# Layer norm, transposes and gate of the last four chunks five passes ahead; the top-k search spread over passes 11 to 15

## The reference

```python
xn = layernorm(x)                                    # eps 1e-5, no scale
# attention: windows of 64 rows, 16 heads of 32
qkv = xw @ qkv_w + qkv_b
attn = softmax(q @ k.T * 32**-0.5 + rel_pos_bias)    # 64 x 64 for each window and head
attention = (attn @ v) @ proj_w + proj_b
# experts: each of the 8 experts picks its own 1024 rows
scores = (xn @ Wg.T).T                               # 8 x 8192
top_vals, token_idx = top_k(scores, 1024)
token_w = softmax(top_vals)
h = silu(xg @ W1.T) * (xg @ W3.T)                    # 1024 x 1024 for each expert
y = (h @ W2.T) * token_w
out = x + attention + scatter_add(y)
```

## Time and profile before

| | us |
|---|---|
| median of 3 runs | 2164.89 (2163.88 to 2164.94) |
| profiled execution | 2163.89 |
| its span | 2162.1 |
| TensorE busy | 2082.4 (96%) |
| VectorE busy | 1101.4 (51%) |
| ScalarE busy | 666.6 (31%) |
| GpSimd busy | 517.9 (24%) |

### The profile page before, as it was taken

How to read it: one execution, slowest core, us unless ns; L and a number is a source line. 1 busy time by engine, 2 the same in 40 slices (tenths; PEclk the granted TensorE clock), 3 DMA queues, 4 the chain that set the end, 5 groups by cost and what they waited for, 6 DMA issues and landing times.

```text
span 2162.1 us, 38085 instructions
## 1 busy us (share of the span) xinstructions
PE 2082.4 (96%) x15667; PEld 1680.8 (78%) x15667; DVE 1101.4 (51%) x1652; ACT 666.6 (31%) x1027; POOL 517.9 (24%) x308
## 2 busy tenths in 40 slices
PE   7999999999999999975799999999999999999997
PEld 5877777787777777754688888888888888888886
DVE  6666666565666666688744433343334433344211
ACT  3333332323232333334323332232232322324221
POOL 2333323333333333213111112111220211201111
PEclk9999999999999999986899999999999999999999
DMA  6121222222122112201333233142331423313311
GB/s 216 45 74 46 79 79 79 78 79 71 56 71 79 60 59 79 78 21 40 118 88 106 59 78 97 41 114 59 74 92 49 108 67 68 88 58 89 66 20 20
DMA packets 65749, 159.21 MB, mean 74 GB/s; under 512 B 5565, under 2 KB 5949, under 8 KB 65693
## 3 DMA queue, kind: packets, MB, share of 16 engines
q1 hardware_dynamic: 51356, 124.93, 17.0%
q0 software_dynamic: 14336, 33.56, 8.7%
HBM read 107.09 MB, written 51.31 MB: 73 GB/s over the span
## 4 chain that ended last, share of the span: by engine, by line
PE 51%; DVE 0%; POOL 0%; ACT 0%; issue 0%; POOLq 0%
PE ps_e L53 16%; PE ps_e L54 16%; PE ps_e L55 16%; PE ps_e L1324 1%; PE ps_e L135 1%; POOL out_rows L1228 0%; DVE xgt_lo L1394 0%; ACT x_res L1296 0%; DVE w_lo L1389 0%; ACT w_hi L1264 0%; POOLq L1227 0%
## 5 line engine op out<-in xcount | busy, mean ns | idle before, releaser
L53 PE MATMUL ps_e<-xgt_hi,w_hi 128*128 128x512 f32 x1024 | 403.7, 394 | 2.8 <-DVE xgt_lo L1394 2.8
L55 PE MATMUL ps_e<-xgt_hi,w_lo 128*128 128x512 f32 x1024 | 398.6, 389 | 0.0
L54 PE MATMUL ps_e<-xgt_lo,w_hi 128*128 128x512 f32 x1024 | 398.5, 389 | 0.0
L1414 DVE TENSOR_TENSOR hm<-ps_e,silu 128x512 f32<-128x512 f32 x128 | 88.5, 691 | 531.3 <-PE ps_e L55 530.6
L53 PEld LDWEIGHTS ps_e<-xgt_hi,w_hi 128*128 128x128 f32 x1024 | 192.2, 188 | 40.9 <-DVE xgt_lo L1394 3.0
L55 PEld LDWEIGHTS ps_e<-xgt_hi,w_lo 128*128 128x128 f32 x1024 | 192.2, 188 | 40.5
L164 POOL DMA_INDIRECT x_in<-xn_rows,idx x64 | 75.7, 1183 | 615.9 <-issue 230.2
L54 PEld LDWEIGHTS ps_e<-xgt_lo,w_hi 128*128 128x128 f32 x1024 | 192.4, 188 | 37.9
L53 PE MATMUL ps<-xt_hi,wqk_hi 128*128 128x512 f32 x512 | 212.0, 414 | 0.0
L1284 ACT ACTIVATE h_hi<-hm 128x512 fp32r<-128x512 f32 x128 | 80.9, 632 | 391.6 <-DVE hm L1414 388.7
L54 PE MATMUL ps<-xt_lo,wqk_hi 128*128 128x512 f32 x512 | 201.5, 394 | 0.0
(11 more groups left out here) (166 smaller groups left out, 3585.0 us busy)
## 6 DMA issues: line engine op xcount, KB each, us to landing
xn<-in_w SPq DMA_DIRECT2D x48, 512.0 KB, 3.3
raw<-in_w SPq DMA_DIRECT2D x48, 512.0 KB
xn_rows<-xn SPq DMA_DIRECT2D x16, 1024.0 KB, 5.2
x_res<-in_x SPq DMA_DIRECT2D x16, 1024.0 KB, 5.0
out_rows<-x_res SPq DMA_DIRECT2D x16, 1024.0 KB, 4.2
x_in<-in_x SPq DMA_DIRECT2D x15, 1024.0 KB, 7.2
x_res<-in_wqk SPq DMA_DIRECT2D x3, 512.0 KB, 6.8
x_in<-in_x SPq DMA_DIRECT2D x2, 512.0 KB, 4.1
```

The source lines that it names most:

```text
L53: nc.tensor.matmul(out, w_hi, x_hi, start=start, stop=False)
L54: nc.tensor.matmul(out, w_hi, x_lo, start=False, stop=False)
L55: return nc.tensor.matmul(out, w_lo, x_hi, start=False, stop=stop)
L1414: v.tensor_tensor(hm[:, m % 2, :], ps[:, 2 * (m % 2) + 1, :], silu[:, m % 2, :], ALU.mult).then_inc(hm_ready, 1)
```

## The change

FAR = 12, LEAD = 5, HUNT = 11. Passes 1 to 6 stay a loop, 7 to 14 are written out. In passes 7 to 10 the norm of chunk c+5 (chunks 12 to 15) is done beside that of chunk c+1, in tiles of its own (`x_f`, `xt_f`), and its transposes and gate (`xt_ahead` in passes 7 to 10, `gate_ahead` in passes 8 to 11, four fp32 matmuls for the former 16); its normed rows are stored, and read back into `xn` one pass before they are transposed again for the projections. Passes 11 to 14 have no norm of their own and passes 12 to 15 no gate. `gate_s`, `above` and the rest lie in the memory of `x_f` and `xt_f`. The search's rounds stand at slots n = 1 to 6 of passes 11 to 13, at the same places of every engine's queue (`hunt(c, n)`); slot n = 7 takes the bits of round n = 6. The banks of the counts change with the slot (SLOT_BANK), and TensorE waits with `bank_free` until VectorE has read them. The choice stands in slot 6 of pass 13 to slot 2 of pass 14, positions and weights in slots 2 to 7 of pass 14, the first list's matmuls between the projections of the last pass, and the gather between two softmax steps of GpSimd there. The last output projection is in two parts, three quarters of it before the last group's probabilities are there. On ScalarE the copies of the odd head pairs in the last pass go to VectorE. Cut to what the prediction speaks of, indented eight columns less:

```diff
+FAR = 12
+LEAD = 5
+HUNT = FAR - 1
+ROUNDS = 16
...
+FINAL_BANK = (7, QB, KB, 2)
+SLOT_BANK = (None, QB, KB, KB, KB, QB, 2)
+TOTAL, WGT_T, LISTS = QB, QB, 7
+def slot(c, n):
+    return 6 * (c - HUNT) + n - 2
...
# SyncE's queue
+    def load_xn_back(c):
+        sp.wait_ge(xn_stored, 16 * FAR)
+        sp.wait_ge(xnf_stored, 16 * (c - FAR + 1))
+        sp.wait_ge(xt_mm, KC * c)
+        sp.dma_start(xn[:, :, :], d["xn"][c]).then_inc(xn_back, 16)
+    def load_terms():
+        sp.wait_ge(gate_stored, 64 * FAR)
+        sp.wait_ge(gatef_stored, 64 * (NCH - FAR))
+        sp.wait_ge(xnf_stored, 16 * (NCH - FAR))
+        for j, term in enumerate((gate_s, above, ties, upto)):
+            sp.dma_start(term, d["gate"][j, :, :]).then_inc(scores_in, 16)
...
+    for c in range(FAR - LEAD, NCH - 1):
+        if c < FAR:
+            keep_scores(c)
+        if FAR <= c - 1 + LEAD < NCH:
+            keep_scores_ahead(c - 1 + LEAD)
+        if c == HUNT:
+            load_terms()
+        if c + 1 < FAR:
+            keep_xn(c + 1)
+        else:
+            load_xn_back(c + 1)
+        if c + 2 < FAR:
+            load_x(c + 2)
+        store_out(c - 1)
+        load_res(c)
+        if c + LEAD < NCH:
+            keep_xn_ahead(c + LEAD)
+        if c + LEAD + 1 < NCH:
+            sp.wait_ge(xnf_stored, 16 * (c + LEAD - FAR + 1))
+            load_x_ahead(c + LEAD + 1)
     sp.wait_ge(xt_mm, KC * NCH)
     for u in range(2):
         sp.dma_start(lists.raw[u], d["w13"][0, u]).then_inc(lists.w_in[u], 16)
+    store_out(NCH - 2)
...
# GpSimd's queue
+        if isinstance(c, int) and FAR <= c + LEAD < NCH:
+            layernorm_rstd_ahead(c + LEAD)
+        if isinstance(c, int) and c == NCH - 2:
+            for j in range(2):
+                pool.wait_ge(wgt_part_ready, j + 1)
+                nc.gpsimd.tensor_tensor(lists.wgt[:, :, :], lists.wgt[:, :, :], lists.wgt_parts[:, :, :, j],
+                                        ALU.subtract).then_inc(wgt_rest_ready, 1)
+        if isinstance(c, int) and c == NCH - 1:
+            pool.wait_ge(xn_ready, TT * FAR)
+            pool.wait_ge(xn_stored, 16 * FAR)
+            pool.wait_ge(xnf_stored, 16 * (NCH - FAR))
+            pool.wait_ge(lists.idx_ready, 1)
+            gather(nc, pool, lists, d["xn_rows"], 0, 0)
         softmax(G * c + 2)
...
# ScalarE: of the new hunt() and chunk()
+        if n <= 6 and 0 <= slot(c, n) < ROUNDS:
+            count_hits(slot(c, n))
+        if c == NCH - 3 and n == 6:
+            act.wait_ge(top_ready, 1)
+            nc.scalar.activation(exps, gate_s, ACT.Exp, bias=top[:, 0:1]).then_inc(exps_ready, 1)
+        if c == NCH - 2 and n == 3:
+            take_weights()
+        if c == NCH - 2 and n in (4, 6, 7):
+            weight_part((4, 6, 7).index(n))
...
# TensorE
+    def xt_ahead(j, k):
+        if k == 0:
+            pe.wait_ge(xnf_ready, TT * (j - FAR + 1))
+            pe.wait_ge(out_ready, TT * (j - LEAD))
+        elif k == 1:
+            pe.wait_ge(s_ready, G * (j - LEAD) + 3)
+        elif k == 3:
+            pe.wait_ge(xtf_ready, KC * (j - FAR) + 1)
+        for t in range(TT):
+            i = nc.tensor.transpose(ps[:, F_BANK[k], P * t:P * (t + 1)], x_f[:, t, P * k:P * (k + 1)], ident[:, :])
+        i.then_inc(xtf_mm, 1)
+    def gate_ahead(j):
+        pe.wait_ge(xtf_ready, KC * (j - FAR + 1))
+        pe.wait_ge(s_ready, G * (j - LEAD + 1))
+        for k in range(KC):
+            i = nc.tensor.matmul(ps[32 * k:32 * (k + 1), GF_BANK, :], wg[:, k, :], xt_f[:, k, :], start=True, stop=True)
+        i.then_inc(gatef_mm, 1)
...
+    def project_out_most(c, t):
+        for k in range(KC - 1):
+            split3(nc, ps[:, FINAL_BANK[t], :], ot_hi[:, k, P * t:P * (t + 1)], ot_lo[:, k, P * t:P * (t + 1)],
+                   wp_hi[:, k, :], wp_lo[:, k, :], k == 0, False)
+    def project_out_rest(c, t):
+        k = KC - 1
+        split3(nc, ps[:, FINAL_BANK[t], :], ot_hi[:, k, P * t:P * (t + 1)], ot_lo[:, k, P * t:P * (t + 1)],
+               wp_hi[:, k, :], wp_lo[:, k, :], False, True).then_inc(p_mm, 1)
...
# TensorE's hunt(c, n)
+        s, i, bank = G * c, slot(c, n), SLOT_BANK[n]
+        if i < 0 or (c == NCH - 2 and n > 3):
+            return
+        if n == 1:
+            pe.wait_ge(q_ready, s + 2)
+        elif n <= 4:
+            pe.wait_ge(k_ready, s + 2)
+        elif n == 5:
+            pe.wait_ge(q_ready, s + 3)
+        else:
+            pe.wait_ge(s_ready, s + 3)
+        if c == NCH - 4 and n in (3, 4):
+            pe.wait_ge(bank_read, i)
+        if i < ROUNDS:
+            pe.wait_ge(part_counts, i + 1)
+            pe.wait_ge(hits_summed, 2 * (i + 1))
+            row_matmul(ps[:, bank, 0:3], same[:, :], cnt[:, :]).then_inc(count_mm, 1)
...
+    def bank_free(c, n):
+        if isinstance(c, int) and HUNT <= c < NCH - 1 and slot(c, n) >= 0:
+            pe.wait_ge(bank_read, slot(c, n) + 1)
     def chunk(c, first=False):
         s = G * c
+        ahead = isinstance(c, int) and FAR <= c + LEAD < NCH
+        late = isinstance(c, int) and c >= FAR
         project_q(s, 0, c)
+        if isinstance(c, int) and FAR < c + LEAD <= NCH:
+            gate_ahead(c - 1 + LEAD)
         if not first:
             probs_t(s - 2)
         project_k(s, 0)
         if not first:
             pv(s - 2, 2)
-            gate(c)
+            if not late:
+                gate(c)
...
         project_q(s + 1, 1)
         if not first:
             project_v(c, 0)
+            hunt(c, 1)
             probs_t(s - 1)
         project_k(s + 1, 1)
         if not first:
...
+        hunt(c, 2)
         project_v(c, 2)
         project_v(c, 3)
+        hunt(c, 3)
         pe.wait_ge(v_ready, TT * c + 3)
         scores(s + 1)
         if not first:
-            for t in range(TT - 1):
-                project_out(c - 1, t)
+            project_out(c - 1, 0)
+            project_out(c - 1, 1)
+            hunt(c, 4)
+            project_out(c - 1, 2)
+        bank_free(c, 1)
+        if isinstance(c, int) and c == NCH - 2:
+            pe.wait_ge(wgt_copied, 1)
         project_q(s + 2, 2)
         probs_t(s)
         pe.wait_ge(v_ready, TT * (c + 1))
+        bank_free(c, 2 if isinstance(c, int) and c == NCH - 2 else 4)
         project_k(s + 2, 2)
         pv(s, 0)
+        hunt(c, 5)
         if not first:
             project_out(c - 1, TT - 1)
             pe.wait_ge(out_ready, TT * (c - 1) + 3)
+        scores(s + 2)
+        if not isinstance(c, int) or c < NCH - 2:
+            bank_free(c, 5)
+        project_q(s + 3, 3)
+        hunt(c, 6)
+        if ahead:
+            for k in range(KC - 1):
+                xt_ahead(c + LEAD, k)
+        probs_t(s + 1)
+        if ahead:
+            xt_ahead(c + LEAD, KC - 1)
+        project_k(s + 3, 3)
+        if ahead:
+            pe.wait_ge(xtf_ready, KC * (c + LEAD - FAR + 1))
+        xt(c + 1)
+        if not isinstance(c, int) or c < NCH - 2:
+            bank_free(c, 6)
+        scores(s + 3)
+        pe.wait_ge(xt_ready, KC * (c + 1) + 1)
+        pv(s + 1, 1)
...
# TensorE's last pass, as it is after
+        def lists_of(*groups):
+            for g in groups:
+                compact(nc, pe, lists, ps[:, LISTS, :], 0, g)
+        project_q(s, 0, c)
+        probs_t(s - 2)
+        project_k(s, 0)
+        pv(s - 2, 2)
+        scores(s)
+        project_q(s + 1, 1)
+        project_v(c, 0, last=True)
+        probs_t(s - 1)
+        project_k(s + 1, 1)
+        pv(s - 1, 3)
+        project_v(c, 1, last=True)
+        project_v(c, 2, last=True)
+        lists_of(0, 1)
+        project_v(c, 3, last=True)
+        lists_of(2)
+        pe.wait_ge(v_ready, TT * (c + 1))
+        scores(s + 1)
+        for t in range(TT):
+            project_out(c - 1, t, last=True)
+            lists_of(3 + t)
+        project_q(s + 2, 2)
+        lists_of(7)
+        probs_t(s)
+        project_k(s + 2, 2)
+        pv(s, 0)
+        pe.wait_ge(out_ready, TT * c)
         scores(s + 2)
         project_q(s + 3, 3)
         probs_t(s + 1)
         project_k(s + 3, 3)
         scores(s + 3)
         pv(s + 1, 1)
+        pe.wait_ge(lists.got_ready, 1)
+        pe.wait_ge(q_ready, G * NCH)
+        pe.wait_ge(k_ready, G * NCH)
         probs_t(s + 2)
         pv(s + 2, 2)
+        pe.wait_ge(o_ready, G * NCH - 1)
         for t in range(TT):
+            project_out_most(c, t)
         probs_t(s + 3)
+        pv(s + 3, 3)
+        pe.wait_ge(o_ready, G * NCH)
         for t in range(TT):
+            project_out_rest(c, t)
...
# VectorE
+    def take_bits(i, bank, top_too=False):
+        dve.wait_ge(count_mm, i + 1)
+        reached = v.tensor_scalar(reach[:, :], ps[:, bank, 0:3], float(CAP), 0.0, ALU.is_ge, ALU.add, accum_out=kept[:, :])
+        if top_too:
+            then(reached)
+        else:
+            then_read(reached, i)
+        then(v.tensor_copy(kept_i[:, :], kept[:, :]))
...
# VectorE's hunt(c, n)
+        i = slot(c, n)
...
```

(75 more changed lines are left out.)

520 lines of the change are left out of this document (261 added, 259 removed).

## The result

The changed kernel takes 2178.74 us (median of 4 runs, 2177.03 to 2181.07), the kernel before 2164.43 (4 runs, 2163.88 to 2164.94): ratio 1.0067, 95% interval 1.0049 to 1.0084. It is slower. The profiled execution took 2177.03 us, its span 2175.3, against a span of 2162.1 before. The expert stage now starts at 1066.56 us instead of 1053.56: the 13.0 us between the two are nearly the whole difference of the spans, 13.2.

What follows compares the result with a forecast made beforehand. TensorE bounds passes 1 to 14; the chain of search, choice and list bounds the last. 2163.9 - 55 + 12 + 2.4 - 5.5 + 7.1 + 33.2 + 21.2 = 2179 us, slower; range 2146 to 2202.

Steps and rivals of the forecast that it cites:

- The last pass, -55: Search, choice and most list waits leave the last pass: 99 us against 153.8, bounds 90 and 108.
- The gap: Last pass: GpSimd gathers between softmax(61) and softmax(62), so TensorE waits 5 us for the normalised tile.
- Passes 7 to 10, +12: The second norm there: 1.84 us of transposes a pass plus waits of 1.15, together 3.0 a pass.
- three of the four gate_ahead: Early gate matmuls in passes 8 to 11, 0.59 us each pass, +2.4 in all; three fall in passes 8 to 10.
- Passes 11 to 14: +56.6: Search matmuls +7.1, gate gone -5.5, slot 2 with clock +33.2, other slots +21.2, and pass 11's gate_ahead.
- The waits at slot 2: Passes 11 to 14: search blocked behind GpSimd's residual addition, 6.6 us in passes 12 and 13; with clock +33.2 in all.
- The other slots: Passes 11 to 13: waits at slots 3, 4, 6, project_q and the pass end, +21.2 us, bounds 0 and 35.
- The clock was forecast at 6.8: Passes 11 to 14: matmuls behind each slot 2 wait run at half clock, 1.7 us a pass.
- The lock: VectorE and GpSimd share a port pair exclusively for a whole instruction; by it the 33.2 us at slot 2 stand.
- rival 1: Faster: the residual addition does not meet the search at slot 2, the 33.2 us vanish, 2146 us; chance 0.27.
- The break-even: Slot 2, passes 11 to 14: below 4.4 us a pass, clock included, the change wins.
- Rival 2: Waits of 1 to 2 us in passes 11 to 13 cost clock too, 24 us more: 2203 us; chance 0.10.

Runs made afterwards that it cites:

- the nine variants above: Nine follow-up variants of the changed kernel, altering or moving its bias addition, comparisons, slot 4, gather or key; medians from 2155.90 to 2181.92 us.
- Experiments 1 to 4: Changed kernel without bias addition in passes 11 to 14, 2164.68 us; addition moved, 2167.68; comparisons over 64 of 512 columns, 2171.08; kernel before without addition, 2164.09.
- the late gather: First list's gather put behind the softmax of group 63 instead of between those of groups 61 and 62; alone on the changed kernel, 2181.92 us.
- two pairs: Gather late against early: with addition moved, slot 4 before maximum, key behind xt_lo, 2155.90 against 2160.07 us; with last-pass additions moved too, 2156.37 against 2160.36.
- the third: Changed kernel with only the gather moved behind the last softmax, 2181.92 us, against the changed kernel, 2178.74.

## Why the prediction was right

The forecast was 2179, the time 2178.74, and most terms stood. That they agree to 0.3 us is luck: the four executions lie between 2177.03 and 2181.07, and several errors of 1 to 5 us cancelled. Step by step:

**The last pass, -55: measured -59.0.** Idle 17.5, busy 77.3 at clock 0.96. Two points failed. The gap was forecast at 5 us before probs_t(62), with TensorE waiting for the normalised tile; it is 3.96 before scores(63), two steps earlier in TensorE's queue, because k's copy shares ScalarE with the exponentials. And the clock: 2 us were allowed, and the nine variants above with much the same waits took 96.7 to 101.0, so that 94.8 is at the low end, and the forecast of 99 is nearer to the other nine than to this one.

**Passes 7 to 10, +12 and three of the four gate_ahead: forecast 13.8, measured 14.9.** They are 62.3, 64.0, 63.6 and 63.6 us instead of 59.65, the last three a little over the forecast's 63.3. The waits forecast at 1.15 were 0.61 (0.20 and 0.41); gate_ahead, sized at 0.6 by four matmuls, took 1.0 (in pass 8 from 487.19 to the next matmul at 488.19, with eight matmuls recorded for the four). Here too two errors cancel in part.

**Passes 11 to 14: +56.6 forecast, +57.7 measured** (79.1, 75.3, 73.2 and 68.7, less four of 59.65). The waits at slot 2 were forecast at 8.0, 6.6, 6.6 and 5.2, together 26.4; they were 7.96, 6.31, 6.06 and 5.93, together 26.3. The row that gave them was 4.09 us of L999 under a residual in the old last pass. The other slots were forecast at 21.2 and are 17.2 (43.5 less 26.3): the end of a pass cost 1.8, not 2.2, and slot 6 1.3. The clock was forecast at 6.8 (1.7 four times). Busy time grew by 14.1. At the forecast's own prices 2.2 of these are work (the search's matmuls 7.1, less the gate 5.5, plus the last gate_ahead 0.6), which leaves 11.9 for the clock. Read directly, in windows of 0.5 us, the clock took about 10.5 (an estimate: TensorE's busy time in each window times what the granted clock lacks of 1.00). It lies in five stretches: 8.8 behind the four waits at slot 2 (1.9, 2.0, 1.8 and 3.0), and 1.7 behind the wait of 1.07 at slot 3 of pass 12:

```profile
793.40:797.40 4.00, 4.00 (x12) 3.09 (x11) 3.90 (x6) 0.00 (x0) 1.63 (x1) 0.57 0.01 2
```

So the two errors, 4 us too much waiting and 4 to 5 too little clock, cancel: luck again.

**The lock.** Experiments 1 to 4 show it: gone when the addition is gone or elsewhere, there with an eighth of the data in the comparisons, of no cost where no search is near. By the Trainium skill, SBUF — State Buffer, section "Who interferes with whom", a VectorE operation with two SBUF inputs and a GpSimd operation that reads SBUF exclude each other for a whole instruction, while one with at most one SBUF input, outside the two-port modes, does not contend. The traces agree on both sides: cand with two SBUF inputs took 4.43 us for its usual 0.16, while s_sum and the copies from PSUM beside the moved addition kept 1.22 and 1.40.

**Where rival 1 was mis-sized.** It said that without the meeting at slot 2 the time is 2146, the whole 33.2 gone. With the addition taken out it was 2164.7. The term bundled three things: the lock (16.7 us of waits), the round's own chain (9.6, which stays), and the clock, of which nothing came back in passes 11 to 14 while the last pass of the profiled execution lost 5. The break-even itself was right: it let slot 2 cost at most 4.4 us a pass of 8.3, so that 3.9 had to go; taking the lock away took 4.2 a pass in waits, and the time came out at that of the kernel before. Rival 2, that short waits cost clock as well, asked for 24 us. In the changed kernel one short wait did, for 1.7. Without the addition its mechanism shows more often: there half clock stands behind waits of 3.78, 1.10, 1.78 and 2.05, and behind the 1.61 and 0.21 at the end of pass 11. The list was ready in time.

**Open:** why the changed kernel's last pass was at 0.96 when kernels with the same idle time were at 0.88 to 0.93, and with it why the late gather gained 4 us in two pairs and nothing in the third. No run here separates the clock from the place of the waits. What the record does show is that executions of one and the same kernel differ in clock: those without the addition took from 2157.50 us at a mean granted clock of 0.994 to 2167.75 at 0.986, those with slot 4 before the maximum from 2174.72 at 0.990 to 2183.96 at 0.983. A difference of 5 us in the last pass of one profiled execution may therefore be no property of the kernel; the medians, 4.2 and 4.0 us apart in the two pairs, rest on 5 to 11 executions each.

## What to carry to other kernels

Before search-like work goes into a stage whose main engine is never idle, list for each slot what the neighbouring queue (here GpSimd) is doing at that time; the free share of VectorE says nothing about it. A GpSimd operation of 4.5 us beside PSUM copies and reductions is free, beside two-input VectorE work that TensorE waits for it costs nearly its whole length (4.2 of 4.5), and a different place in the same queue mends that without removing any work: four changes of order turned 0.67% slower into 0.35% faster. And count waits and clock apart: idle time taken away comes back at once, busy time stretched by the clock may not.
